# A gated delta layer's block solve, with its products multiplied on VectorE and summed on TensorE, and three moves around it

## The reference, cut to what matters

```python
def step(S, inp):
    qt, kt, vt, at, bt = inp                      # at, bt: sigmoids, one number per head and token
    Sk = jnp.einsum('bhde,bhe->bhd', S, kt)
    S_new = at * S - at * bt * Sk[..., :, None] * kt[..., None, :] + bt * vt[..., :, None] * kt[..., None, :]
    ot = jnp.einsum('bhd,bhde->bhe', qt, S_new)
    return (S_new, ot)
```

## Time and profile before

| | us |
|---|---|
| median of 3 runs (lowest, highest) | 1884.42 (1880.28, 1885.7) |
| the profiled execution, its own time | 1883.49 |
| its span, first to last instruction | 1881.8 |
| busy: PE / PEld / DVE / ACT / POOL | 1266.9 / 779.3 / 1434.8 / 973.7 / 351.4 |
| first experts' block to the rows back in place | 851.5 to 1062.5 |
| projection and convolution | 1066.8 to 1157.5 |
| solve | 1157.5 to 1293.4 |
| scan | 1293.4 to 1515.5 |
| output | 1521.3 to about 1680 |

### The profile page before, as it was taken

How to read it: one execution, slowest core, us unless ns; L and a number is a source line. 1 busy time by engine, 2 the same in 40 slices (tenths; PEclk the granted TensorE clock), 3 DMA queues, 4 the chain that set the end, 5 groups by cost and what they waited for, 6 DMA issues and landing times. The chain is left out here.

```text
span 1881.8 us, 42023 instructions
## 1 busy us (share of the span) xinstructions
PE 1266.9 (67%) x15746; PEld 779.3 (41%) x15746; DVE 1434.8 (76%) x2661; ACT 973.7 (52%) x2042; POOL 351.4 (19%) x495
## 2 busy tenths in 40 slices
PE   4689999999999999991599483000000049950998
PEld 2225555555555555451599342000000014430997
DVE  4689999898999989824265485999989979871564
ACT  4638888788888888864266372201222200031564
POOL 6101000000100000005335200000000025536055
PEclk9869999999999999995699785555555569975999
DMA  3521111111111100022312254610221110011222
GB/s 95 172 55 31 31 31 32 31 31 31 31 31 40 40 14 3 3 69 70 77 13 27 54 143 110 179 45 11 68 64 39 40 50 1 1 45 50 53 23 25
DMA packets 99034, 92.16 MB, mean 49 GB/s; under 512 B 21745, under 2 KB 82994, under 8 KB 98450
## 3 DMA queue, kind: packets, MB, share of 16 engines
q1 hardware_dynamic: 83106, 78.18, 16.4%
q0 software_dynamic: 11264, 8.92, 3.3%
q10 hardware_dynamic: 4464, 2.38, 0.5%
HBM read 47.28 MB, written 31.21 MB: 42 GB/s over the span
## 5 line engine op out<-in xcount | busy, mean ns | idle before, releaser
L725 DVE TENSOR_REDUCE att_negmax<-att_ps_max 128x1 f32<-128x1024 f32 x512 | 621.4, 1223 | 74.4 <-PE att_ps_max L595 45.3
L713 ACT ACTIVATE att_probs<-att_ps_prob 128x512 f32<-128x512 f32 x1024 | 556.3, 595 | 135.6 <-PE att_ps_prob L610 132.3
L595 PE MATMUL att_ps_max<-av_k_op,av_q_op 81*32 81x512 bf16 x4096 | 416.5, 394 | 10.9 <-PEq L104 7.2
L610 PE MATMUL att_ps_prob<-av_q_op,av_k_op 99*32 99x512 bf16 x4096 | 410.3, 383 | 2.1 <-DMA av_q_op<-att_nm_parts 0.4
L627 PE MATMUL att_ps_acc<-att_probs,att_vq 128*32 128x256 f32 x4096 | 315.1, 379 | 0.0
L1985 PE MATMUL out_ps_y<-all_bo_row,all_ones 1*128 1x128 f32 x2 | 0.8, 482 | 361.0 <-PEq L104 361.0
L1118 PE MATMUL moe_moe_ps_up<-moe_moe_xgT,moe_moe_wbuf 128*128 x1456 | 196.8, 279 | 0.0
L1118 PEld LDWEIGHTS moe_moe_ps_up<-moe_moe_xgT,moe_moe_wbuf 128*128 128x128 f32 x1456 | 181.4, 196 | 0.1
L595 PEld LDWEIGHTS att_ps_max<-av_k_op,av_q_op 81*32 81x32 bf16 x4096 | 115.5, 97 | 129.6 <-DVE att_negmax L725 28.2
L610 PEld LDWEIGHTS att_ps_prob<-av_q_op,av_k_op 99*32 99x32 bf16 x4096 | 107.7, 95 | 142.0 <-ACT att_probs L713 83.9
L627 PEld LDWEIGHTS att_ps_acc<-att_probs,att_vq 128*32 128x32 f32 x4096 | 133.3, 111 | 77.0 <-issue 0.5
(11 more groups left out here) (278 smaller groups left out, 1768.7 us busy)
## 6 DMA issues: line engine op xcount, KB each, us to landing
av_k_op<-terms_k SPq DMA_DIRECT2D x48, 216.0 KB
av_q_op<-terms_q SPq DMA_DIRECT2D x144, 72.0 KB
solve_dec_and_windows<-solve_Xw SPq DMA_DIRECT2D x16, 256.0 KB, 3.0
solve_dec_and_windows<-b_k_lane SPq DMA_DIRECT2D x16, 256.0 KB, 3.7
moe_moe_xs<-expert_rows SPq DMA_DIRECT2D x6, 576.0 KB, 6.6
terms_q<-qkv_parts_q SPq DMA_DIRECT2D x8, 384.0 KB, 3.1
terms_k<-qkv_parts_k SPq DMA_DIRECT2D x8, 384.0 KB, 3.3
all_w_all<-in_f_w SPq DMA_DIRECT2D x24, 128.0 KB, 2.5
```

The costliest lines, as they stand in the source:

```text
L595: mm = pe.matmul(ps_max[c * STRIP:(c + 1) * STRIP, n % 2, k * CH:(k + 1) * CH], q_op[s][0:R_ALL, qt // CT, h, at:at + STRIP], k_op[s][0:R_ ...
L610: mm = pe.matmul(ps_prob[c * STRIP:(c + 1) * STRIP, j % 2, :], k_op[s][0:R_END, h, at:at + STRIP], q_op[s][0:R_END, half, h, :], start=Tru ...
L713: act.activation(probs[:, j % PROBS, :], ps_prob[:, j % 2, :], ACT.Exp).then_inc(s_exp, 1)
L725: dve.tensor_reduce(negmax[:, w % 2, a:a + 1], ps_max[:, n % 2, :], AX.X, ALU.max, negate=True).then_inc(s_maxed, 1)
```

## The change

The solve is written anew, and three things around it move.

1. **Layout by place.** ScalarE turns k, v, gates and scale so that a tensor holds [place t in the block, channel, block c], 512 contiguous numbers per place, in the memory of `b_q`, `b_k`, `b_a`; at the end it turns w and v back (L2023). The gates' running products (`whole`, `rest`) are made by place, 64 numbers each.
2. **VectorE multiplies, TensorE sums.** For place t, `multiply_M(t)` writes k_j times k_t for up to four j into one of three `slots`; TensorE multiplies them with the identity and sums the eight channels in a PSUM bank (`sum_M`). `weigh_M(t)` makes the weights and multiplies them in. `multiply_X` writes unknown j times M[j, t] for w and v into slots, `sum_X` sums over j in a PSUM bank, and one `subtract` per place and side makes the unknown. M is multiplied four places ahead. w and v advance together.
3. **In the solve's block** the norms' DMAs go from ScalarE to SP; the loads of a, q and k by channel go behind the first two windows' loads; the sigmoid of `a` goes to the output block, one batch at a time. `xv`, `p1` and `p2` of the scan lie in slot 0.
4. **v's lanes late:** in the convolution v of batch b-1 is loaded at the head of batch b, and v of the last batch at the head of the solve's block.
5. **Experts behind slots:** in `moe`, `places` runs before `experts_of_tiles`; and in the first experts a row's DRAM place is lane x 32 + tile, so that a lane's rows are contiguous.

The diff, cut to its core:

```diff
-        resid_tiles = resid.rearrange("(t p) c -> p t c", p=P)
+        resid_tiles = resid.rearrange("(p t) c -> p t c" if out is None else "(t p) c -> p t c", p=P)
...
             pair_totals()
+            places()
             experts_of_tiles()
-            places()
...
             for b in range(B):
+                if b:
+                    load_rows(b - 1, 2, g.v_lane, g.s_vlane)
                 store_gates(b)
                 store_rows(b, 0)
-                if b:
-                    load_rows(b - 1, 2, g.v_lane, g.s_vlane)
...
-            load_rows(B - 1, 2, g.v_lane, g.s_vlane)
             sp.wait_ge(s_out[1], 16 * B)
+            sp.wait_ge(s_out[2], 16 * B)
...
+SLOTS = 3
+SLOT = 4
+EARLY_M = 4
...
+            def sum_M(n, t, j0, j1):
...
+                for e in range(D):
+                    mm = pe.matmul(ps_M[(t - 1) % EARLY_M][:, j0 * LB:j1 * LB], g.ident[:, :],
+                                   slot_of(n, j0, j1)[:, :, e, :], start=(e == 0), stop=(e == D - 1))
+                mm.then_inc(s_used, 1)
+
+            def sum_X(n, w, t, j0, j1):
+                wait_used(pe, s_solved[w], t - 2)
+                pe.wait_ge(s_prod, n + 1)
+                for j in range(j0, j1):
+                    mm = pe.matmul(ps_X[w][t % 2][:, :], g.ident[:, :],
...
+                                   start=(j == 0), stop=(j == t - 1))
+                mm.then_inc(s_used, 1)
...
+            for t in range(1, L):
+                weigh_M(t)
+                if early(t):
+                    for w in range(2):
+                        multiply_X(w, t, 0, early(t))
+                if t > 1:
+                    for w in range(2):
+                        subtract(w, t - 1)
+                for w in range(2):
+                    multiply_X(w, t, early(t), t)
+                start_X(t)
+                if t + EARLY_M < L:
+                    multiply_M(t + EARLY_M)
+                if t == L - 4:
+                    dve.wait_ge(s_ks, 16 * NL)
+                    in_order(k_scale[:, :]).then_inc(s_scaled, 1)
+                if t == L - 2:
...
+                    in_order(to_end[:, :]).then_inc(s_kready, 1)
+            for w in range(2):
+                subtract(w, L - 1)
...
+            for t in range(L):
+                for w, (dst, done) in enumerate(((Xw4, s_wready), (Xv4, s_ready))):
...
+                    ins = act.activation(dst[:, t], Xt[w][:, t, :, :], ACT.Copy)
+                    if t == L - 1:
+                        ins.then_inc(done, 1)
```

More of the change, by code:

```diff
@@ L1639, in solve_and_scan @@
+        ps_norm = ps_M[EARLY_M - 1][:, 0:P]
         s_norm = m.sem("norm")
@@ L1789, in _ @@
-            dve.tensor_copy(byblock(to_end[:, :]), dec[:, :, :, L - 1].rearrange("p i c -> p c i")).then_inc(s_chain, 1)
-            chain.n = chain.n + 1
-            chain.done(dve.tensor_tensor(w3, dec[:, 0, :, :], a3[:, :, 0:1].to_broadcast([P, LB, L]), ALU.mult))
-            dve.tensor_copy(end[:, :], w3[:, :, L - 1])
-            for i in range(L - 1):
-                ins = dve.tensor_tensor(dec[:, i, :, i + 1:], dec[:, i, :, i + 1:], b3[:, :, i + 1:], ALU.mult)
-            chain.done(ins)
@@ new lines, in _ @@
+            dve.wait_ge(s_sig, 2)
+            dve.tensor_copy(whole[:, 0, :], at[:, 0, :]).then_inc(s_chain, 1)
+            dve.memset(rest[:, L - 1, :], 1.0).then_inc(s_chain, 1)
+            chain.n = 2
+            dve.wait_ge(s_chain, 2)
+            for t in range(1, L):
+                dve.tensor_tensor(whole[:, t, :], whole[:, t - 1, :], at[:, t, :], ALU.mult).then_inc(s_chain, 1)
+                i = L - 1 - t
+                dve.tensor_tensor(rest[:, i, :], rest[:, i + 1, :], at[:, i + 1, :], ALU.mult).then_inc(s_chain, 1)
+                chain.n = chain.n + 2
+                dve.wait_ge(s_chain, chain.n)
@@ new lines, in _ @@
+            dve.tensor_copy(end[:, :], whole[:, L - 1, :]).then_inc(s_rest, 1)
+            multiply_M(EARLY_M)
+            dve.wait_ge(s_st, 1)
+            chain.done(dve.tensor_tensor(bs, bt[:, :, :], st[:, :, :], ALU.mult))
+            dve.wait_ge(s_rest, 1)
+            chain.done(dve.scalar_tensor_tensor(out=whole[:, :, :], in0=whole[:, :, :], scalar=-1.0, in1=bs,
+                                                op0=ALU.mult, op1=ALU.mult))
+            start_X(0)
+            dve.wait_ge(s_first, 2)
@@ L1842, in body @@
+            for w in range(2):
+                subtract(w, L - 1)
+            dve.wait_ge(s_one, 1)
             def body(i):
@@ L1895, in _ @@
+            for t in range(EARLY_M):
+                turn_lanes(kt, k, t, s_kt)
             act.wait_ge(g.s_ablane, 16 * NL)
[L1896 to L1901 removed]
@@ new lines, in _ @@
+            act.wait_ge(s_ks, 16 * NL)
+            act.activation(st[:, :, :], in_turn(k_scale[:, :]), ACT.Copy).then_inc(s_st, 1)
+            for t in range(1, L):
+                if EARLY_M + t < L:
+                    turn_lanes(kt, k, EARLY_M + t, s_kt)
+                turn_lanes(Xvt, Xv, t, s_vt)
+            act.wait_ge(s_rest, 1)
+            act.activation(in_turn(to_end[:, :]), rest, ACT.Copy).then_inc(s_toend, 1)
+            Xw4 = Xw[:, :, :].rearrange("p (c t) e -> p t e c", t=L)
@@ L2096, in _ @@
         def _(act):
+            for b in range(B):
+                tok = slice(b * S, (b + 1) * S)
+                act.activation(a[:, tok], a[:, tok], ACT.Sigmoid).then_inc(s_a, 1)
             for b in range(B):
```

253 lines of the change are left out of this document (150 added, 103 removed).

## The result

| | before | changed |
|---|---|---|
| median, us (lowest, highest) | 1882.91 (1880.28, 1885.7) | 1853.68 (1852.47, 1855.31) |
| span of the profiled execution | 1881.8 | 1850.6 |

A forecast was written before the change was run, and what follows sets the result against it. VectorE was taken to bound the solve, and the DMA queue the convolution's end. Gains of 17.3 + 3.8 + 3.0 + 0.6 = 24.7 us took the span from 1881.8 to 1857.1, the execution to 1858.8, say 1859; range 1850 to 1876.

The forecast's parts named there:

- the solve with its tail: Solve up to the scan's start: 25.0 us gained by VectorE's end, 7.7 lost behind it, 17.3 in sum.
- VectorE's end: End of VectorE's work in the solve: 104.7 us after the norm rows instead of 129.7, 25.0 gained.
- ScalarE: Solve's start: VectorE waits for the sigmoids behind table loads, root and turns of k; 0.8 us charged.
- the first term: Solve: VectorE's waits for TensorE's sums at full clock, 5.5 us: about 3 at the end, 2.5 in places 2 to 4.
- the second: Solve: TensorE's low clock, places 1 to 3 mostly at half speed; 6 us charged, between nothing and 12.
- The clock: Sign in the solve: TensorE's granted clock at 1.00 in most of the stretch from 20 us after the block's start.
- The rival in which it goes up and down: Solve: TensorE's clock averages 0.67, a unit takes 1.28 us, time 1868 us; chance 0.2.
- The tail: VectorE's end to the scan: first window behind both windows' w and k, 10.7 us instead of 3.0, 7.7 lost.
- TensorE as the bound: Solve: clock stays low, 84 units take 143.6 us at 1.2 GHz, slower, 1902 us; chance 0.08.
- v's late loads: Convolution's end: v's last loads leave the bounding DMA queue and SP's issuing; 3.8 us gained, bounds 1.2 and 4.
- Slots first: Both experts' blocks: POOL's scatter no longer waits behind the tiles' experts; 3.0 us gained for both.
- Rows by lane: Rows' way back from the first experts: packets grow from 512 B to 4 KB; 0.6 us gained, nothing to 1.6.

The follow-up runs named there:

- the solve alone: Changed kernel with the three moves (v's last lanes, slots first, rows by lane) taken back; 1862.93 us, ratio 0.9896 to the kernel before.
- the experiment with few sums: Changed kernel with one matmul for each piece of products, some 30 of 84 units of sums staying; 1843.01 us, one execution.
- all sums twice: Changed kernel with every matmul of the sums issued twice into the same bank, 168 units instead of 84; 1907.78 us, one execution.
- the windows first: Changed kernel with SP loading k of both windows early, then w and v of the first window, then those of the second; 1847.39 us, ratio 0.9791.
- the decays early: Kernel with k in quarters, plus the first two windows' four decay loads issued behind k's stores, before w is ready; 1840.71 us, ratio 0.9776.
- k scaled in the gaps: Changed kernel, first window's w, k, v loaded first, k's second scaling in two halves ahead of the last two subtractions; 1844.03 us, ratio 0.9785.
- in quarters: Kernel with k scaled in the gaps, plus k's first scaling in four pieces of 1024 numbers in places 2 to 5; 1841.69 us, ratio 0.978.

## Why the prediction was right

**The sign and the size** held: 1859 us were predicted, 1853.7 measured, in the range. Of the 4.9 us between 24.7 and 29.6, the scan's jumps, 4.6, are in no term of it; the rest is small errors that cancel, and in the profiled pair some 3 us of the convolution's clock against 2.3 us lost ahead of the experts. The jumps, the convolution's clock and the cancelling are luck; the solve with its tail, 17.3 predicted, 16.4 in the stages and 15.2 in those of the solve alone, is not.

**VectorE's end**, 104.7 us after the norm rows, came at 1256.79 - 1152.57 = 104.2. By terms: work 92.4 predicted, 104.2 less the waits' 13.6, so 90.6 measured. *ScalarE* 0.8 predicted, 2.4 measured: a turn of 512 numbers takes 1.04 us (four in 4.17), above the upper bound of 0.92 that was taken from an eighth of the long copy, so the bounds did not hold; a sigmoid with the same turn takes 1.15. *TensorE* 5.5 + 6 predicted, 11.2 in the waits, 11.5 in the experiment with few sums. The waits can be read one by one. Up to place 4, at full clock, they are 3.3 us where 2.5 were predicted. In place 5, where the clock had fallen, it is 2.2. In place 7 they are 5.8; by the 2.3 us that its sums took beyond 12.0, some 3.5 of these would have come at full clock, where 3 were predicted. That is an estimate of 6.7 us for the first term and 4.5 for the second. But the second was charged for a slow start in places 1 to 3, and there VectorE waited for no sum while the clock was low: the first wait for one ends at 1176.10, the clock was at 1.00 from 1165 on, and TensorE had stood idle for 2.1 us ahead of those sums, so no backlog of the slow start was left. All of the clock's cost came from the two later falls. That 6 us was near is luck.

**The clock** was 0.50 until 1160, 0.95 over the next 5 us and then 1.00, so it rose some 11 us after the block's start, sooner than the 20 us given. The rival in which it goes up and down happened twice, for some 10 and 5 us, and cost 2 to 3 us each. It was described as falls between short groups; they came behind VectorE's two longest instructions, which the working had costed as VectorE's time alone. One group shows that the idle time just before does not decide alone: the sums for M of place 5 follow 2.1 us of idle time in all of these kernels, and took 5.42 us in the changed one, with the solve alone, the windows first and the decays early, but 7.11, at a clock of 0.76, in the experiments with k scaled in the gaps and in quarters. The rule of the Trainium skill ("TensorE: Matmul & The Clock Gate", A second HAM failure mode: psum-queue depth-cycling), by which small idle times between groups throttle the clock again and again, agrees with the 0.76 and not with the 1.00 over the same row in the changed kernel.

**The tail**: 7.7 us lost predicted, 9.1 measured. From w's ready to the scan 12.5 were taken, and 1268.90 - 1255.35 = 13.55 measured; w's lead on VectorE's end was 1.4 instead of 1.8. Its mechanism, a first window behind loads that it does not need or that could have come earlier, is shown by the experiment with the windows first. The 6 MB by channel cost nothing, as said: no third window waited.

**TensorE as the bound** was the slower rival. With all sums twice the clock stayed high once it had risen, so it was right to give that case little; but its price of 0.855 us a unit was too low by 8% (0.93), M's narrow matmuls and the slow start together.

**The three moves.** v's late loads 3.8 predicted, at least 4.2 in the last batch of every kernel that has them, 5.3 (3.6 to 7.0) as a ratio: in the stages the upper bound of 4 did not hold. The larger part is the one that was worked out from bytes in the queue, 2.6 us: from the last batch's gates' store to the landing of its last store of v it is 14.8 to 15.6 us in the five kernels with v in the old place and 11.3 to 12.2 in the nine others, 3.4 less in the mean. Slots first 3.0 predicted, some 2 measured: the wait that took its place, ScalarE's rows, was overlooked, though in the trace of before ScalarE's last rows ended at 869.92, 1.8 us ahead of the scatter. Rows by lane 0.6 predicted, 2.4 in its stages: 1.1 on the way back, since SP issues the four loads in 1.76 us instead of 3.98 and the statistics run without gaps, and 1.3 in the experts, where the rows are also stored and added to, which was not taken apart; only the first place had been counted. The upper bound of 1.6 did not hold. By the Trainium skill's rule on 512 B ("DMA: Bandwidth & Descriptors", Specifications) this term would be nothing; the ratio, 0.9983 with an upper end of 0.9991, speaks against it here, and so do the transfers themselves. The 2 MB come as 4096 packets of 512 B before and as 512 of 4 KB with the rows by lane, and in the middle of them the engines move 269 and 336 GB/s; the last packet ends 8.9 and 7.7 us after SP began to issue:

```profile
1055.00:1060.00 5.00, 0.00 (x0) 0.00 (x0) 4.59 (x23) 0.00 (x0) 0.00 (x0) 0.50 1.11 269
```
```profile
1054.00:1058.00 4.00, 0.00 (x0) 0.00 (x0) 3.74 (x20) 0.00 (x0) 0.00 (x0) 0.50 0.86 336
```
(the kernel before; the rows by lane)

**Two signs** that the prediction named came out otherwise: the solve's block starts 8.1 us earlier and not 6, and POOL's first scatter 0.95 earlier and not 1.5. The others held.

## What to carry to other kernels

When VectorE adds up what it multiplied, TensorE with an identity matrix can do the adding, if the sums are taken early enough that only the last ones are waited for; but every long instruction of VectorE that yields no products is then a gap for TensorE, and its clock can fall behind it, which is paid for a second time. Such an instruction can go to where VectorE waits anyway, which brought VectorE's end 4.4 us forward here but cost 2.4 in the tail, since the loads of k wait for it; it should not go to GpSimd. When three results become ready at once, order their loads by what the consumer needs first: that gained 6 to 10 us, more than any of the three moves. And before two kernels are compared, look for stalls that neither of them means to change: one instruction more was worth 4 us here.

## What was not expected of the hardware

- Two engines, one at a time: a GpSimd multiplication of 4096 numbers (8.88 us) held a VectorE instruction of 0.69 us for 9.39.
- The second and third jump back of the scan's loop cost VectorE 5.0 to 5.2 us each in the kernels with its instruction list of before, and 2.7 to 3.0 in all others, two of which have one instruction more. This was 4.6 us, 0.25% of the kernel, as much as many a deliberate change is worth. The first jump cost 0.27 us with the old solve, whatever the other two were.
- The third batch of the convolution takes 19.1 or some 16.2 us, also in kernels with the same code there, at a granted clock of 0.76 or 0.90 in the two shown.
- Places 5 and 6 of the solve, with the same code and the same gaps of 3.3 and 2.3 us in front of them, lost TensorE's clock in place 6 in one profiled execution (8.82 and 12.23 us for places 5 and 6) and in place 5 in another (10.52 and 10.54).
- SP's issuing has no fixed price: the same two loads of v took 1.30 us with the windows first, 1.99 with k in quarters and 2.46 with the decays early. What holds it was not looked into.
